# A fused attention and FFN layer: LN3's VectorE work reordered, 35 FFN products ahead of the slots instead of 30, and step 0's weight preparation and K stacking redistributed

## The chip, the cores and the metric

One core of one Trainium2 chip. TensorE is PE in the profile, its weight loads PEld, VectorE DVE, ScalarE ACT, GpSimd POOL, SyncE SP (SPq where its queue of DMAs is meant). The metric is the time of one launch on the device in microseconds (us); lower is better.

## What is computed

```python
x = L0_attn_hidden_states                                  # 16 x 512 x 512
x = x + _layernorm(_L0_attn_ref(_layernorm(x), ...))
x = x + _layernorm(_L0_ffn_ref(_layernorm(x), ...))
# attention: q = x @ Wq_down.T @ Wq_up.T, c = x @ Wkv_down.T, k and v from c per head (16 heads of 32),
#            scores * SCALE - slope * |i - j|, causal, softmax, @ v, @ Wo.T
# FFN:       weights are 4-bit codes times fp16 group scales; h = silu(x @ Wg.T) * (x @ Wu.T); y = h @ Wd.T; y / rms(y)
```

## The kernel before

Every fp32 operand is split into a high and a low fp16 part, and a product is three matmuls (high x high, high x low, low x high) that accumulate in one PSUM bank. ACT writes the high part ("high"), DVE the rest ("low", line 873).

The program is a row of steps, `step(t)` for t = 0 to 16. Step t does the attention of sequence t (`att`) and the FFN of sequence t - 1 (`ffn`); step 0 has attention alone, step 16 FFN alone, steps 1 to 15 have both. All engines run hand-written queues in a fixed order; semaphores join them.

The head of a step, on PE: transposes of the input, the output projection WO of the sequence before, C (the 128-wide latent), Q0 and Q1, K0 to K3, Q2 and Q3, V0 and V1, then the transposes of LN3's result (line 433), V2 and V3, then the first `F_FIRST` = 30 products of the FFN's up matrices (`run(0, cut(0))`). The jobs from C to V share four PSUM banks (`wide_dense`): a job opens when the job four before it has been read (`open_job`, `taken`), so Q2 waits for K0's low and Q3 for K1's. On DVE the head is: low parts of the input, LN2's moments and x1 = x + LN2 (line 972), Q0 and Q1 low, then four times LN3's `bn_stats` (line 982) ahead of a K low, the aggregation and the request for 1/sqrt (`ask_rstd`, answered by POOL, line 1080), Q2 and Q3 low, the four norms (line 788), and the low parts of their transposes. SP stacks Q and K for the slots with DMAs: 12 for the first half of Q once Q1's low is there, then 12 for K, then 12 for the rest of Q (line 1195). The FFN's jobs F0, F1, ... (12 products each, gate and up alternating) rotate through three banks: `gate(m)` frees the bank of gate job 2m, `up(m)` that of up job 2m+1, and a job opens when the one three before it is free.

After the head come 64 slots (`SLOTS`). A slot has score tiles for row maxima (`maximum`, line 505) or transposed score tiles for the exponentials (`transposed`, line 522) and a share of the FFN's products: `cut(slot)` spreads what is left after `F_FIRST` by the weights `PER_SLOT`. The slots in which ACT, DVE and POOL do `tanh(m)`, `gate(m)`, `up(m)`, `h_high` and `h_low` follow from `cut` through `up_done` and `down_done`: `tanh(m)` stands one slot behind the one that finishes its job, `gate(m)` two behind. In slot 16 ACT also takes the logarithm of the first half of the row sums, which loads an ACT table before and after; in slot 18 DVE splits the result (`lse_split`). The same comes again in slots 40 and 42.

Step 0 also prepares weights. `prepare` makes Wq from its factors; `decode(0)` turns the gate/up codes into fp8 on DVE (two masks, an OR, two masks, an OR, and the scales, on 128x1408 words), `decode(1)` does the same with the down codes (128x704), `decode_wo` makes Wo's low half. 33 `unit`s then expand the codes: POOL multiplies codes by scales (line 1090), PE transposes (line 365), ACT or DVE writes the high and DVE the low half. Nine units stand ahead of the slots of step 0, the other 24 in its slots 0 to 39.

## Time and profile before

| | us |
|---|---|
| median of 3 runs (lowest to highest) | 2552.22 (2552.08 to 2552.81) |
| the profiled execution, whole | 2549.71 |
| its span on the core | 2547.8 |
| PE busy (mean granted clock 0.985) | 2445.3 |
| DVE busy | 1523.3 |
| ACT busy | 1465.3 |
| POOL busy | 591.6 |

PE is busy for 96% of the span, so the view to read is what PE waits for, stage by stage. Matmuls are pipelined and their ends are modelled: 12 matmuls in a row start 0.216 us apart, and the last one's listed end lies some 0.16 us behind the point at which the next could start. A wait is therefore best taken from start to start.

### The profile page before, as it was taken

The page shows a single profiled execution, that of the slowest core. Times are in us where ns is not written, and L with a number is a line of the kernel's source. Part 1 is how long each engine was busy: PE and PEld are TensorE (multiplying, and loading weights), DVE is VectorE, ACT ScalarE, POOL GpSimd, SP SyncE. Part 2 cuts the span into 40 slices and gives each one's busy share as a digit, 9 for nine tenths or more (in the row PEclk, how much of TensorE's full clock was granted, in tenths as well). Part 3 has the DMA queues.
Part 4 walks back from the last instruction along what each step waited for, and adds up shares of the span by engine and source line. Part 5 has one row for each costly group of instructions (what it writes and reads, how often), then busy time and mean ns, then how long its engine had stood idle before and what let it go on. Part 6 is the DMA issues. An engine that isn't in the chain of part 4 may idle for free.

```text
span 2547.8 us, 38721 instructions
## 1 busy us (share of the span) xinstructions
PE 2445.3 (96%) x13372; PEld 1112.6 (44%) x13372; DVE 1523.3 (60%) x4300; ACT 1465.3 (58%) x3927; POOL 591.6 (23%) x648
## 2 busy tenths in 40 slices
PE   6689999999999999999999999999999999999988
PEld 3334444444444444444444444444444444444433
DVE  6856475565646657575665647556564665657442
ACT  3756556474664747566474655747566474756610
POOL 3312313123131221313122131312213122131312
PEclk9699999999999999999999999999999999999999
DMA  5020121201112020121202012120111202012000
GB/s 138 23 49 19 51 50 34 67 18 42 43 43 59 25 72 11 46 50 35 67 18 62 22 51 50 35 67 18 42 43 43 59 24 74 8 48 50 19 17 17
DMA packets 99521, 108.89 MB, mean 43 GB/s; under 512 B 22895, under 2 KB 73199, under 8 KB 99311
## 3 DMA queue, kind: packets, MB, share of 16 engines
q1 hardware_dynamic: 99326, 106.44, 15.9%
q8 instruction: 105, 1.72, 0.3%
q14 instruction: 90, 0.74, 0.1%
HBM read 38.49 MB, written 16.78 MB: 22 GB/s over the span
## 4 chain that ended last, share of the span: by engine, by line
PE 80%; DVE 7%; ACT 5%; SPq 3%; issue 2%; DMA 1%; POOL 1%; DVEq 0%; POOLq 0%
PE dense L338 58%; PE psO L538 6%; PE score L522 4%; SPq L1195 3%; PE psO L338 3%; PE low L505 3%; PE score L505 3%; DVE st_ln L777 2%; ACT arena L719 1%; PE low L522 1%; DVE arena L873 1%; DMA kst<-arena 1%; DVE low L1024 1%; ACT L650 1%; ACT L719 1%
## 5 line engine op out<-in xcount | busy, mean ns | idle before, releaser
L338 PE MATMUL dense<-arena,wgu 128*128 128x512 f16 x4224 | 999.9, 379 | 11.4 <-DVE late L886 10.2
L338 PEld LDWEIGHTS dense<-arena,wgu 128*128 128x128 f16 x4224 | 405.3, 97 | 445.2 <-DVE late L886 17.5
L338 PE MATMUL dense<-wdn,arena 128*128 128x512 f16 x2112 | 533.0, 380 | 2.6 <-POOL arena L1109 2.6
L1109 POOL TENSOR_TENSOR arena<-late,arena 128x512 f16<-128x512 f32 x176 | 203.4, 1156 | 1050.8 <-DVE arena L907 1050.8
L1024 DVE CUSTOM_DVE_ANT_0 low<-low,mmax 128x128 f32<-128x128 f32 (+3 forms) x672 | 278.7, 435 | 260.8 <-PE low L505 257.9
L719 ACT ACTIVATE arena<-score 128x512 f32<-128x512 f32 (+3 forms) x720 | 302.4, 440 | 188.6 <-PE score L522 142.2
L644 ACT ACTIVATE low<-low,ncol 128x128 f32<-128x128 f32 (+3 forms) x672 | 300.1, 447 | 136.7 <-DVE ncol L1024 128.4
L644 ACT ACTIVATE score<-score,ncol 128x384 f32<-128x384 f32 x352 | 214.0, 608 | 169.8 <-DVE ncol L1024 169.4
L338 PEld LDWEIGHTS dense<-wdn,arena 128*128 128x128 f16 x2112 | 199.2, 98 | 186.7 <-issue 11.5
L1024 DVE CUSTOM_DVE_ANT_0 score<-score,mmax 128x384 f32<-128x384 f32 x352 | 214.2, 649 | 100.3 <-PE score L505 100.0
L522 PE MATMUL score<-qst,kst 128*128 128x512 f16 (+3 forms) x784 | 218.6, 306 | 13.8 <-ACT arena L719 12.6
L1122 POOL TENSOR_SCALAR_AFFINE_SELECT arena<-arena 128x512 f32<-128x512 f32 x240 | 165.6, 690 | 280.6 <-ACT arena L719 278.7
L912 DVE TENSOR_SCALAR arena<-oc 128x512 f16<-128x512 f32 x64 | 27.3, 426 | 272.2 <-ACT oc L638 272.2
L538 PE MATMUL psO<-arena 128*32 128x512 f32 (+3 forms) x1920 | 178.7, 444 | 3.7 <-ACT oc L638 1.6
L505 PE MATMUL low<-kst,qst 125*128 125x128 f16 (+3 forms) x672 | 156.3, 277 | 12.9 <-ACT low L644 9.5
L886 DVE SCALAR_TENSOR_TENSOR late<-late,dense 128x512 f32<-128x512 f32 x176 | 120.5, 684 | 57.1 <-ACT late L629 55.8
L1024 DVE DVE_READ_ACCUMULATOR2_ANT ncol<- 128x1 f32 x1024 | 145.2, 142 | 0.2
L629 ACT ACTIVATE late<-dense 128x512 f32<-128x512 f32 x176 | 103.7, 589 | 67.3 <-PE dense L338 67.3
L894 DVE SCALAR_TENSOR_TENSOR late<-late,dense 128x512 f32<-128x512 f32 x176 | 120.3, 684 | 32.6 <-PE dense L338 32.6
L719 ACT ACTIVATE arena<-low 128x384 f32<-128x384 f32 (+3 forms) x240 | 104.3, 435 | 51.1 <-PE low L522 51.1
L644 ACT ACTIVATION_READ_ACCUMULATOR low<-low,ncol 128x1 f32 x672 | 133.2, 198 | 0.0
L522 PEld LDWEIGHTS score<-qst,kst 128*128 128x128 f16 x784 | 72.0, 98 | 138.2 <-ACT arena L719 61.1
(138 smaller groups left out, 2874.2 us busy)
## 6 DMA issues: line engine op xcount, KB each, us to landing
qst<-arena SPq DMA_DIRECT2D x384, 64.0 KB, 2.1
kst<-arena SPq DMA_DIRECT2D x192, 128.0 KB, 2.5
xin<-x SPq DMA_DIRECT2D x16, 1024.0 KB, 5.2
late<-x SPq DMA_DIRECT2D x64, 256.0 KB, 2.8
out<-late SPq DMA_DIRECT2D x64, 256.0 KB, 2.0
qst<-mrow SPq DMA_DIRECT2D x96, 8.0 KB, 1.9
wgu<-wo_t SPq DMA_DIRECT2D x1, 1024.0 KB, 7.8
wgu<-wq_down SPq DMA_DIRECT2D x1, 768.0 KB, 4.5
```

Source lines behind the costliest of these rows:

```text
L338: ins = nc.tensor.matmul(dst, w, a, start=first and k == 0, stop=last and k == len(tt) - 1)
L505: nc.tensor.matmul(mx_bank(k)[:, 0:P * (i + 1)], qst[0:P - 3, h, P * i:P * i + P], kst[0:P - 3, h, 0:P * (i + 1)], start=True, stop=True). ...
L522: ins = nc.tensor.matmul(st_bank(e)[:, 0:wide], kst[:, h, P * kt:P * kt + P], qst[:, h, P * kt:L], start=True, stop=h >= STEEP)
L538: ins = nc.tensor.matmul(psO[HD * a:HD * a + HD, P * kt:L], v[:, kt, HD * (HG * g + a):HD * (HG * g + a) + HD], prob_of(s)[:, a, 0:wide], ...
L629: nc.scalar.activation(tb[:, m % 2, :], bank(t, n)[:, :], ACT.Tanh, scale=0.5 / (S_X * S_W4)).then_inc(sem["tanh"], 1)
L644: nc.scalar.activation(mx_bank(k)[:, 0:wide], mx_bank(k)[:, 0:wide], ACT.Exp, scale=-1.0, bias=ncol[:, k:k + 1], accum_out=scol[:, k:k + 1 ...
L719: nc.scalar.activation(prob_of(e // HG)[:, e % HG, 0:wide], st_bank(e)[:, 0:wide], ACT.Exp, scale=1.0 / S_SCORE).then_inc(sem["exp"], 1)
L886: nc.vector.scalar_tensor_tensor(tb[:, m % 2, :], tb[:, m % 2, :], 1.0, bank(t, n)[:, :], ALU.add, ALU.mult).then_inc(sem["freev"], 1)
L894: nc.vector.scalar_tensor_tensor(tb[:, m % 2, :], tb[:, m % 2, :], S_H / (2 * (S_X * S_W4) ** 2), bank(t, n)[:, :], ALU.mult, ALU.mult).th ...
L1024: nc.vector.tensor_tensor_reduce(out=mx_bank(k)[:, 0:wide], in0=mx_bank(k)[:, 0:wide], in1=mmax[:, L - wide:L], scale=-1.0 / S_SCORE, scal ...
L1109: nc.gpsimd.tensor_tensor(ht[:, 1, m, :], tb[:, m % 2, :], ht[:, 0, m, :], ALU.subtract).then_inc(sem["hl"], 1)
L1122: nc.gpsimd.affine_select(out=diagonal, in_=diagonal, compare_op=ALU.is_ge, fill=0.0, base=0, pattern=[[0, HG], [1, P]], channel_multiplie ...
```

## The change

In the steps that have both halves, DVE's order changes: LN3's first two `bn_stats` stand behind Q0's low and ahead of Q1's, the third behind K0's low, the fourth behind K1's; the aggregation and the request for 1/sqrt follow at once, ahead of K2's low; the four norms stand behind Q2's low and ahead of Q3's. `F_FIRST` is 35 instead of 30.

In step 0, the decoding of the gate/up codes is cut in three: the first mask pair and OR behind the input's low parts, the second pair of masks behind C's low, the second OR and the scales behind Q0's low. The decoding of the down codes (`decode_down`) moves from the head into slot 4. Wo's low half is made by POOL in two instructions ahead of its first unit, and is no longer on DVE. The first loads are issued in another order (down codes, gate/up codes, Wo, gate/up scales, down scales). K is stacked by two queues: SP issues heads 0 and 1 of each group of four, ACT heads 2 and 3, behind its K highs and a wait for K3's low.

```diff
-F_FIRST = 30
+F_FIRST = 35
...
+        def stack(queue, dst, hi, slots, lo_g, hi_g, heads, done):
+            for slot, s in enumerate(slots):
+                for a in heads:
+                    queue.dma_start(
+                        dst[HD * slot:HD * slot + HD, :, :].rearrange("p (g a) l -> p g a l", a=HG)[:, lo_g:hi_g, a, :],
+                        qk[HD * a:HD * a + HD, hi + s, lo_g:hi_g, :]).then_inc(sem[done], 16)
...
+                    if isinstance(t, int) and t == 0:
+                        taken(act, t, j["K"] + NG - 1)
+                        stack(nc.scalar, kst, 2, (0, 0, 1), 0, NG, range(2, HG), "kstk")
                     for g in range(2, NG):
                         high(job_q(t, g), qk[:, 0, g, :], HD ** -0.5 * S_QK / (S_X * S_WQ))
...
-                decode(0)
                 for c in range(KC):
                     dve.wait_ge(s_prep_hi, c + 1)
...
-            def decode_wo():
-                dve.wait_ge(s_raw_hi, 4)
-                nc.vector.scalar_tensor_tensor(wo[:, 1, :, :].rearrange("p a b -> p (a b)"), raw[:, 9 * D:13 * D], S_W,
-                                               wo[:, 0, :, :].rearrange("p a b -> p (a b)"),
-                                               ALU.mult, ALU.subtract).then_inc(s_raw_lo, 1)
...
                 if isinstance(t, int) and t == 0:
-                    decode(1)
+                    decode(0)
...
                     low("C", 0, ct[:, 1, :], S_C / (S_X * S_W), ct[:, 0, :])
+                if isinstance(t, int) and t == 0:
+                    decode(1)
...
-                if att:
-                    for g in range(2):
-                        low("Q", g, qk[:, 1, g, :], HD ** -0.5 * S_QK / (S_X * S_WQ), qk[:, 0, g, :])
-                for g in range(NG):
-                    if ffn:
-                        dve.wait_ge(sem["add2"], val("add2", t, g + 1))
-                        link(t, nc.vector.bn_stats(st6["ln3"][:, g, :], x1[:, g, :]))
-                    if att:
-                        low("K", g, qk[:, 3, g, :], S_QK / (S_C * S_W), qk[:, 2, g, :])
-                if ffn:
+                if att:
+                    q_low(0)
+                if isinstance(t, int) and t == 0:
+                    decode(2)
+                if ffn:
+                    for i in range(2):
+                        ln3_stats(i)
+                if att:
+                    q_low(1)
+                    k_low(0)
+                if ffn:
+                    ln3_stats(2)
+                if att:
+                    k_low(1)
+                if ffn:
+                    ln3_stats(3)
                     aggregate(t, "ln3", range(NT))
                     ask_rstd("ln3")
                 if att:
-                    if isinstance(t, int) and t == 0:
-                        decode_wo()
                     for g in range(2, NG):
-                        low("Q1", g - 2, qk[:, 1, g, :], HD ** -0.5 * S_QK / (S_X * S_WQ), qk[:, 0, g, :])
+                        k_low(g)
+                if att:
+                    q_low(2)
                 if ffn:
                     dve.wait_ge(sem["rs"], val("rs", t, 2))
                     for i in range(NT):
                         normalise("ln3", xn2[:, i, :], x1[:, i, :], i).then_inc(sem["ln3"], 1)
+                if att:
+                    q_low(3)
...
+                    if isinstance(t, int) and t == 0 and slot == 4:
+                        decode_down()
...
             def unit(u):
-                pool.wait_ge(s_bits, 7 if u < 2 * MI else 14)
+                pool.wait_ge(s_bits, 7)
+                if u >= 2 * MI:
+                    pool.wait_ge(s_dbits, 7)
+                if u == 0:
+                    pool.wait_ge(s_wo_lo, 1)
...
                 if isinstance(t, int) and t == 0:
+                    pool.wait_ge(s_raw_hi, 4)
+                    flat = raw[:, 9 * D:13 * D]
+                    nc.gpsimd.tensor_scalar(flat, flat, S_W, None, ALU.mult).then_inc(s_wo_s, 1)
+                    pool.wait_ge(s_wo_s, 1)
+                    nc.gpsimd.tensor_tensor(wo[:, 1, :, :].rearrange("p a b -> p (a b)"), flat,
+                                            wo[:, 0, :, :].rearrange("p a b -> p (a b)"), ALU.subtract).then_inc(s_wo_lo, 1)
                     for u in range(RING):
                         unit(u)
...
+                        own = 2 if done == "kstk" and isinstance(t, int) and t == 0 else HG
+                        stack(nc.sync, dst, hi, slots, lo_g, hi_g, range(own), done)
```

On DVE, the head of step 1 (the same in steps 1 to 15; `dense` and `psO` are the banks of the jobs, `st_ln`, `mv_ln`, `ve_ln` LN3's moments, `arena<-late,mv_ln,rs_ln` its norm). Before, from K0's low on:

```order
242 L873 SCALAR_TENSOR_TENSOR arena<-psO,arena 128x512
243 L982 BN_STATS st_ln<-late 128x6
244 L873 SCALAR_TENSOR_TENSOR arena<-dense,arena 128x512
245 L982 BN_STATS st_ln<-late 128x6
246 L873 SCALAR_TENSOR_TENSOR arena<-dense,arena 128x512
247 L982 BN_STATS st_ln<-late 128x6
248 L873 SCALAR_TENSOR_TENSOR arena<-dense,arena 128x512
249 L784 BN_AGGR mv_ln<-st_ln 128x2 x4
250 L879 TENSOR_SCALAR ve_ln<-mv_ln 128x4
251 L873 SCALAR_TENSOR_TENSOR arena<-psO,arena 128x512
252 L873 SCALAR_TENSOR_TENSOR arena<-dense,arena 128x512
253 L788 TENSOR_SCALAR arena<-late,mv_ln,rs_ln 128x512 x4
```

After, from the first two `bn_stats` on (the rows ahead are x1's and Q0's low):

```order
240 L1011 BN_STATS st_ln<-late 128x6 x2
241 L897 SCALAR_TENSOR_TENSOR arena<-dense,arena 128x512
242 L897 SCALAR_TENSOR_TENSOR arena<-psO,arena 128x512
243 L1011 BN_STATS st_ln<-late 128x6
244 L897 SCALAR_TENSOR_TENSOR arena<-dense,arena 128x512
245 L1011 BN_STATS st_ln<-late 128x6
246 L800 BN_AGGR mv_ln<-st_ln 128x2 x4
247 L903 TENSOR_SCALAR ve_ln<-mv_ln 128x4
248 L897 SCALAR_TENSOR_TENSOR arena<-dense,arena 128x512 x2
249 L897 SCALAR_TENSOR_TENSOR arena<-psO,arena 128x512
250 L804 TENSOR_SCALAR arena<-late,mv_ln,rs_ln 128x512 x4
251 L897 SCALAR_TENSOR_TENSOR arena<-dense,arena 128x512
```

The aggregation moved ahead of K2's and K3's low, and the norms (x4) ahead of the last low of Q.

On DVE around slots 16 to 18 of step 1, where LSE is split (rows of `lcol` and `mh`). L886 is `gate`, L894 `up`, L907 `h_high`, the ISA rows row maxima. Before:

```order
344 L1024 ISA score,ncol<-score,mmax 128x512
345 L1024 ISA ncol 128x1
346 L1024 ISA low,ncol<-low,mmax 128x128
347 L1024 ISA ncol 128x1
348 L1024 ISA low,ncol<-low,mmax 128x256
349 L1024 ISA ncol 128x1
350 L922 TENSOR_TENSOR lcol<-ncol,lcol 128x32
351 L924 TENSOR_SCALAR mh<-lcol 128x32
352 L926 SCALAR_TENSOR_TENSOR lcol<-lcol,mh 128x32
353 L929 TENSOR_SCALAR mh<-lcol 128x32
354 L931 TENSOR_TENSOR mh<-lcol,mh 128x32
355 L886 SCALAR_TENSOR_TENSOR late<-late,dense 128x512
```

After (L910 is `gate`, L918 `up`):

```order
342 L1071 ISA score,ncol<-score,mmax 128x512
343 L1071 ISA ncol 128x1
344 L910 SCALAR_TENSOR_TENSOR late<-late,dense 128x512
345 L1071 ISA low,ncol<-low,mmax 128x128
346 L1071 ISA ncol 128x1
347 L1071 ISA low,ncol<-low,mmax 128x256
348 L1071 ISA ncol 128x1
349 L946 TENSOR_TENSOR lcol<-ncol,lcol 128x32
350 L948 TENSOR_SCALAR mh<-lcol 128x32
351 L950 SCALAR_TENSOR_TENSOR lcol<-lcol,mh 128x32
352 L953 TENSOR_SCALAR mh<-lcol 128x32
353 L955 TENSOR_TENSOR mh<-lcol,mh 128x32
```

`gate(6)`, which stood behind the split in slot 18, now stands in slot 17, ahead of slot 18's tiles; on ACT its `tanh(6)` moves from slot 17 to slot 16, ahead of the table loads.

On DVE in step 0, from the low halves of the small weights on. Before (L831 to L840 are `decode`, L809 Wq's low, L873 the lows of the input and of C):

```order
9 L805 SCALAR_TENSOR_TENSOR vup<-wgu,vup 128x512
10 L831 TENSOR_SCALAR arena<-arena 128x1408
11 L832 TENSOR_SCALAR arena<-arena 128x1408
12 L834 TENSOR_TENSOR late<-arena 128x1408
13 L836 TENSOR_SCALAR arena<-arena 128x1408
14 L837 TENSOR_SCALAR arena<-arena 128x1408
15 L839 TENSOR_TENSOR late<-arena 128x1408
16 L840 TENSOR_SCALAR late<-arena 128x88
17 L809 SCALAR_TENSOR_TENSOR wq<-dense,wq 128x512 x3
18 L809 SCALAR_TENSOR_TENSOR wq<-psO,wq 128x512
19 L873 SCALAR_TENSOR_TENSOR arena<-low,arena 128x512 x2
20 L873 SCALAR_TENSOR_TENSOR arena<-score,arena 128x512 x2
```

After:

```order
10 L824 SCALAR_TENSOR_TENSOR wq<-dense,wq 128x512 x3
11 L824 SCALAR_TENSOR_TENSOR wq<-psO,wq 128x512
12 L897 SCALAR_TENSOR_TENSOR arena<-low,arena 128x512 x2
13 L897 SCALAR_TENSOR_TENSOR arena<-score,arena 128x512 x2
14 L833 TENSOR_SCALAR arena<-arena 128x1408
15 L834 TENSOR_SCALAR arena<-arena 128x1408
16 L836 TENSOR_TENSOR late<-arena 128x1408
17 L897 SCALAR_TENSOR_TENSOR ct<-psO,ct 128x512
18 L839 TENSOR_SCALAR arena<-arena 128x1408
19 L840 TENSOR_SCALAR arena<-arena 128x1408
20 L897 SCALAR_TENSOR_TENSOR arena<-dense,arena 128x512
21 L843 TENSOR_TENSOR late<-arena 128x1408
```

The input's lows no longer stand behind a decode, and C's low now stands behind the first piece of it.

## Rows read from the trace of the kernel before

**Rows 1.** Busy time, slots of step 0: span, PE, PEld, DVE, ACT, POOL; PE clock, DMA, GB/s.

```profile
60.10:155.70 95.60, 67.77 (x379) 32.48 (x380) 67.86 (x202) 71.59 (x215) 35.34 (x40) 0.75 0.11 31
```

**Rows 2.** Waits of PE, whole span: engine, line, whom for; us, times, longest.

```profile
PE low L433 <- DVE arena L788: 20.5, 16, 10.9
PE score L522 <- ACT arena L719: 12.6, 22, 3.1
PE dense L338 <- DVE late L886: 10.2, 15, 0.7
...
PE low L505 <- DMA kst<-arena: 3.2, 7, 0.7
```

**Rows 3.** Timeline, head of step 7: start, us, engine, line, out<-in, xcount [idle <-releaser].

```profile
1083.31 2.11 PE L338 MATMUL dense<-ct,kup 128*128 128x512 f16 x9
...
1083.57 0.69 DVE L873 SCALAR_TENSOR_TENSOR arena<-dense,arena 128x512 f16<-128x512 f32 x1 [1.17 <-PE psO L338]
...
1084.28 7.71 SPq L1195 DMA_DIRECT2D qst<-arena  x12
...
1085.51 2.76 PE L338 MATMUL psO<-arena,wq 128*128 128x512 f16 x12
...
1089.59 1.01 POOL L1080 TENSOR_TENSOR rs_ln<-ve_ln,half 128x4 f32<-128x4 f32 x1 [11.34 <-DVE ve_ln L879]
...
1090.69 1.46 PE L338 MATMUL dense<-vup,ct 128*128 128x512 f16 x6
...
1092.04 8.53 SPq L1195 DMA_DIRECT2D kst<-arena  x12
1092.20 1.91 DVE L788 TENSOR_SCALAR arena<-late,mv_ln,rs_ln 128x512 f32<-128x512 f32 x4
...
1092.80 0.44 PE L433 MATMUL low<-id,arena 128*128 128x128 f32 x2 [0.64 <-DVE arena L788]
...
1096.07 6.63 PE L338 MATMUL dense<-arena,wgu 128*128 128x512 f16 x30
```

**Rows 4.** Timeline, slot 18 of the same step.

```profile
1138.32 1.89 PE L338 MATMUL dense<-arena,wgu 128*128 128x512 f16 x8
...
1139.34 0.59 ACT L629 ACTIVATE late<-dense 128x512 f32<-128x512 f32 x1
...
1140.14 0.68 DVE L886 SCALAR_TENSOR_TENSOR late<-late,dense 128x512 f32<-128x512 f32 x1
...
1140.88 0.39 PE L338 MATMUL dense<-arena,wgu 128*128 128x512 f16 x1 [0.68 <-DVE late L886]
```

**Rows 5.** Timeline, step 0 ahead of its slots.

```profile
18.68 0.89 DVE L831 TENSOR_SCALAR arena<-arena 128x1408 int32<-128x1408 int32 x1
...
22.55 1.94 ACT L672 ACTIVATE wo<-wgu 128x2048 f16<-128x2048 f32 x1
...
25.33 0.20 DVE L840 TENSOR_SCALAR late<-arena 128x88 f32<-128x88 f16 x1
...
30.23 0.52 DVE L831 TENSOR_SCALAR arena<-arena 128x704 int32<-128x704 int32 x1
30.37 5.19 PE L338 MATMUL psO<-arena,wkv 128*128 128x512 f16 x12 [8.51 <-DVE arena L873]
...
33.95 0.18 DVE L840 TENSOR_SCALAR late<-arena 128x44 f32<-128x44 f16 x1
...
51.99 1.50 PE L365 MATMUL dense<-id,arena 128*128 128x128 f32 x12 [0.89 <-ACT arena L692]
```

**Rows 6.** Timeline, VectorE and GpSimd on SBUF at once, end of step 1.

```profile
281.46 1.95 DVE L788 TENSOR_SCALAR xin<-xin,mv_ln,rs_ln 128x512 f32<-128x512 f32 x2
281.62 1.50 POOL L1115 TENSOR_TENSOR late<-late 128x512 f32<-128x512 f32 x1 [0.68 <-DVE late L954]
```

**Rows 7.** Groups of POOL by form: line, op, names, shapes, xcount, busy us, mean ns, idle.

```profile
L1109 POOL TENSOR_TENSOR arena<-late,arena 128x512 f16<-128x512 f32 x176 | 203.4, 1156 | 1050.8 <-DVE arena L907 1050.8
L1122 POOL TENSOR_SCALAR_AFFINE_SELECT arena<-arena 128x512 f32<-128x512 f32 x240 | 165.6, 690 | 280.6 <-ACT arena L719 278.7
```

More of the change, by code:

```diff
@@ L234, in layer_program @@
         s_dn = ctx.enter_context(nc.semaphore("s_dn"))
+        s_dn_sc = ctx.enter_context(nc.semaphore("s_dn_sc"))
+        s_dbits = ctx.enter_context(nc.semaphore("s_dbits"))
+        s_wo_s = ctx.enter_context(nc.semaphore("s_wo_s"))
+        s_wo_lo = ctx.enter_context(nc.semaphore("s_wo_lo"))
         s_id = ctx.enter_context(nc.semaphore("s_id"))
@@ L375, in step @@
                 if isinstance(t, int) and t == 1:
[L377 removed]
+                    pe.wait_ge(s_wo_lo, 1)
                     pe.wait_ge(s_prep_lo, KC + UNITS)
@@ new lines, in decode_down @@
+            def decode_down():
+                ts = nc.vector.tensor_scalar
+                words, low3, sign = packed[:, GUW:W], bits1[:, 0:DNW], packed[:, 0:DNW]
+                dve.wait_ge(s_dn, 16)
+                dve.wait_ge(s_bits, 7)
+                ts(low3, words, 0x07070707, 2, ALU.bitwise_and, ALU.logical_shift_left).then_inc(s_dbits, 1)
+                ts(sign, words, 0x08080808, 4, ALU.bitwise_and, ALU.logical_shift_left).then_inc(s_dbits, 1)
+                dve.wait_ge(s_dbits, 2)
+                nc.vector.tensor_tensor(codes[:, 0, GUW:W], low3, sign, ALU.bitwise_or).then_inc(s_dbits, 1)
+                dve.wait_ge(s_dbits, 3)
+                ts(low3, words, 0x70707070, 2, ALU.bitwise_and, ALU.logical_shift_right).then_inc(s_dbits, 1)
+                ts(sign, words, -0x7F7F7F80, None, ALU.bitwise_and).then_inc(s_dbits, 1)
+                dve.wait_ge(s_dbits, 5)
+                nc.vector.tensor_tensor(codes[:, 1, GUW:W], low3, sign, ALU.bitwise_or).then_inc(s_dbits, 1)
+                dve.wait_ge(s_dn_sc, 16)
+                ts(sc32[:, 2 * MI * GROUPS:NSC], sc16[:, 2 * MI * GROUPS:NSC], FP8_SCALE * S_W4, None,
+                   ALU.mult).then_inc(s_dbits, 1)
@@ L1192, in step @@
                         taken(sp, t, last)
-                        for slot, s in enumerate(slots):
-                            for a in range(HG):
-                                sp.dma_start(
-                                    dst[HD * slot:HD * slot + HD, :, :].rearrange("p (g a) l -> p g a l", a=HG)[:, lo_g:hi_g, a, :],
-                                    qk[HD * a:HD * a + HD, hi + s, lo_g:hi_g, :]).then_inc(sem[done], 16)
+                        own = 2 if done == "kstk" and isinstance(t, int) and t == 0 else HG
+                        stack(nc.sync, dst, hi, slots, lo_g, hi_g, range(own), done)
                     for part in range(2):
```

53 lines of the change are left out of this document (29 added, 24 removed).

## The prediction

> **What bounds the kernel now.** I read the waits of PE over the span first [rows 2], then the timeline of one middle step, then step 0 by itself. PE works nearly all the time, so what the change can give is what PE waits, and the waits have a pattern. The one for LN3's norm and the one for a gate come in each of the 15 double steps (the norm's 10.9 us in the last step, which has no attention, is a 16th), the one for an exponential comes once a step too, and the wait for K's stack comes 7 times, 3.2 us in all, one of them in step 0. Step 0 is another matter: in its slots DVE is busy 67.86 of 95.60 us and PE runs at a mean granted clock of 0.75, so PE does not set its end [rows 1]. In the first third of those slots DVE has hardly a gap, later ACT is as busy.
>
> I cost each wait from start to start, with 0.216 us from one product to the next (a row of 12 lists 2.76 with a modelled tail of some 0.16 [rows 3]).
>
> **The double steps: LN3.** The two first `bn_stats` go where DVE stood idle for 1.17 us ahead of Q1's low [rows 3]. In the old order each of these and each low took 0.60 us of DVE, so two need 1.19: Q1's low stays where it is, at 1083.57, and so does the start of SP's stacking at 1084.28. K0's low then follows at 1084.17, not at 1084.86. PE had nine K products from 1083.31, so Q2 could open at 1085.25 and opened at 1085.51 [rows 3]. Gain (a): 0.26 us.
> The aggregation waits for the fourth `bn_stats` right behind it, which the K3 low used to cover; I charge 0.1. K2's and K3's lows come some 0.1 us later than before, which nobody feels: V0 and V1 want them three us later, and SP is busy with Q's 12 DMAs until 1092.04. The request for 1/sqrt goes out at 87.2, POOL answers in 1.01 us [rows 3], so at 88.3. Q2's product ends 0.26 earlier, ACT copies it, its low runs 88.8 to 89.4, and the norms 89.4 to 91.3 (1.91 for four [rows 3]). PE arrives with V0 and V1 done at 1090.69 + 6 x 0.216 - 0.26 = 1091.72 and finds all four. Before, it could have come at 1091.98 and started at 1092.80. Gain (b): 0.82 us. What is late next: Q3's low (about 91.3 to 91.9), wanted by V3 at 94.2, so nothing.
>
> **The double steps: 35 products ahead.** PE is now 1.08 us earlier at the head's end, but K's stack is not: SP's chain of 7.71 and 8.53 us starts at the same point [rows 3]. Five products more take 5 x 0.216 = 1.08, so PE meets slot 0 where it did, and the occasional waits for K's stack stay what they were. Without the five, the gain of (a) and (b) would be handed back there; this edit has no price of its own but is their cover.
> It also shifts the slots. Product 180 opens F15 and needs `gate(6)`. That gate runs at 1140.14 because tanh(6), queued behind ACT's table loads, ends only at 1139.9 and the LSE split stands ahead of it; PE could have gone on at 1138.32 + 8 x 0.216 = 1140.05 and did at 1140.88 [rows 4]. With the new `cut`, job 12 ends one slot earlier, tanh(6) stands in slot 16 ahead of the loads and the gate in slot 17, over an us before PE wants it. Gain 0.83. Next late is F16, now the first product of slot 20 while `up(6)` stands in slot 19: by the pattern of a slot with the wide tiles that is a tie, for which I take off 0.08. Gain (c): 0.75 us.
> Against it: ahead of the first pair of tiles in slot 42 PE waits 0.54 for an exponential behind the second table load (15 of the 22 waits of that name [rows 2]). Slot 40 has one product less now, so that wait grows. Loss (d): 0.2 us.
> Sum: 0.26 + 0.82 + 0.75 - 0.2 = 1.63, times 15 = 24.4 us. Step 16 has no attention, its order of LN3 does not change and neither does its 10.9.
>
> **Step 0, the head.** The input's lows no longer stand behind a decode of 6.9 us (18.68 to 25.53 [rows 5]): they end near 23.9 (30.37 less 6.9, and half a us since ACT's copies then come last), and PE starts C there. The idle time ahead of C shrinks from 8.51 us to 2. C's 12 products took 5.19 us, the same number takes 2.76 elsewhere [rows 3, 5]; that is the lower of the two clocks after a long idle stretch. I take 2.6 for them now. Everything from there follows some 9 us earlier if DVE keeps pace: the first unit's transposes at 43.6 instead of 51.99 [rows 5], since nine units of POOL's pace then follow in both versions, and K's stack (6 DMAs on each queue, about 0.7 us each) is there before they end.
> But DVE may not keep pace. POOL now works 128x2048 elements twice, from the end of ACT's Wo copy at 24.5 [rows 5] on. No trace shows these forms at this size; by the nearest rows, 128x512 takes 0.69 with one input and 1.16 with two [rows 7], times four 2.8 and 4.6, together 7.4 us (I stay with that; up to 9.2 if both run at the two-input rate). In the same time DVE's decode pieces run from SBUF to SBUF, 6.9 us of them. And such pairs do not overlap here: at 281.46 two norms, 0.48 us each where four take 1.91 [rows 3], took 1.95, since the second ran only after POOL's addition of 1.50 that lies between [rows 6]. So I serialise: masks, POOL's scaling 24.8 to 27.5, a mask, POOL's subtraction 28.3 to 32.9, and the OR behind it to 34.6. C's low, queued behind that OR, is 7 us late (35.2); K0 waits for it, PE has done C and Q0, Q1 (36 products) by 31.7 and idles to 35.2, DVE has two masks, Q0's low, an OR and Q1's low to do, and K3's low ends near 42.2. ACT then issues six DMAs (0.64 each by SP's 7.71 for 12 [rows 3]: 3.9 us), in front of Q2's high. V's last copy ends near 49.8 and the units start at 49.9: of 8.4 us gained 2.1 remain.
> The Trainium skill states this as a rule in "SBUF — State Buffer", section "Who interferes with whom": VectorE in a two-port mode or with two SBUF inputs and GpSimd take one shared pair of ports in turn, for a whole instruction each. Without it the head would give 8.4 us, with it 2.1; the row at 281.46 agrees with the rule, and my sum goes by that row.
>
> **Step 0, the slots.** `decode_down` used to run 30.23 to 34.13, 3.9 us [rows 5], beside PE's C product: free. Now it stands in slot 4, where DVE is the bound, so all of it counts, and one unit of POOL (two inputs, 1.1 us by [rows 7]) gets between its pieces: 5.0 us, bounds 3.9 and 6.
> Sum of step 0: -2.1 + 5.0 = 2.9 us slower; between 4.5 faster (no contention: 8.4 - 3.9) and 6 slower.
>
> **Forecast.** -24.4 + 2.9 = -21.5. Against the profiled execution's 2549.71 that is 2528.2; the median lies 2.5 above it (2552.22), so 2530.7, say 2531 us.
>
> **Rivals.**
> A: VectorE and GpSimd do not hinder each other in the head of step 0. For it: units and VectorE's row maxima run side by side in the slots. Against it: [rows 6]. Step 0 gives 4.5 instead of costing 2.9: 2523.3 us.
> B: the gate's wait does not go but moves, to F16 or to another job that the new cuts bring to the edge. For it: F16 is a tie, and this wait was itself one slot's shift away. Against it: no other job came near a wait before. It costs (c), 11 us: 2542.
> C: LN3 gives nothing, because the head's end is K's stack after all: its last DMA sometimes hangs (six of the 15 double steps wait), and PE's gain turns into longer waits at slot 0. It takes (a) and (b), 16 us: 2547.
> D, slower: the two `bn_stats` push Q1's low. Their 1.19 us against an idle 1.17 has no slack; SP's chain starts on that low, and each us of delay is an us of idle PE at slot 0 in 15 steps. It outweighs the gains from a delay of 1.43 us on (24.4 - 2.9 = 21.5 over 15 steps), that is if a `bn_stats` took 1.3 instead of 0.6; at 1.8 us of delay the time is 2531 + 27 = 2558. Nothing in the profile shows such a duration.
> E: no change, for instance if POOL's 1/sqrt comes late so that (b) stays and F16 takes (c) while step 0 costs 6: within 5 us of 2552.
>
> **How the numbers follow.** Forecast 0.51, A 0.20, B 0.14, C 0.07, D 0.04, E 0.04. What a measurement can tell from no change is 0.2%, 5 us. Faster: 0.92; same 0.04; slower 0.04. The range takes in A at the lower end with an us or two for step 0's unknown durations, and B at the upper one: 2521 to 2543.
>
> **What the changed profile would show.** (a) and (b): no wait of PE for the norm in steps 1 to 15, only the last step's 10.9. (c): no wait for the gate in slot 18; one of under 0.1 in slot 20 at most. (d): the wait for the exponential at some 0.75. K's stack: still a wait in about six steps. Double steps 1.6 us shorter each. Step 0: decode pieces stretched or displaced where POOL's two long instructions run, PE idle ahead of K0, units from about 50 us, and a block of some 5 us of decode in slot 4. I am wrong if the double steps shrink by under a us, if Q1's low and with it SP's first stack start later against the head's products, or if the ORs start at once beside POOL.

## The result and the profile after

The changed kernel takes 2531.47 us (2530.07 to 2532.58), the kernel before 2552.15 on the same chip: a ratio of 0.992, with a 95% interval of 0.9903 to 0.9937. The forecast was 2531. The profiled execution took 2531.45 us, its span is 2528.9 against 2547.8.

The waits of PE over the whole span after the change (engine, line, whom for; us, times, longest):

```profile
PE score L534 <- ACT arena L735: 17.1, 22, 3.1
PE score L517 <- ACT score L656: 13.3, 15, 4.9
PE low L445 <- DVE arena L804: 10.9, 1, 10.9
...
PE dense L350 <- DVE arena L897: 5.6, 3, 3.9
...
PE low L517 <- DMA kst<-arena: 3.5, 9, 0.9
```

Against [rows 2]: the wait for LN3's norm has gone from 16 times to once, the last step's. The row for the gate is no longer there. The wait for an exponential rose from 12.6 to 17.1, K's stack from 3.2 to 3.5. Two more changed, both in step 0. The 5.6 us for low parts are new. The wait for a score bank (L517, `row_sum` on ACT) was 8.3 us before:

```profile
PE score L505 <- ACT score L644: 8.3, 13, 2.2
```

It is 13.3 now, 4.9 of it at once, behind a row maximum that came late.

The head of step 7 (start, us, engine, line, out<-in, count, idle and who ended it):

```profile
1079.18 2.11 PE L350 MATMUL dense<-ct,kup 128*128 128x512 f16 x9
...
1079.44 0.69 DVE L897 SCALAR_TENSOR_TENSOR arena<-dense,arena 128x512 f16<-128x512 f32 x1
...
1080.16 7.71 SPq L307 DMA_DIRECT2D qst<-arena  x12
...
1081.12 2.75 PE L350 MATMUL psO<-arena,wq 128*128 128x512 f16 x12
...
1085.22 1.91 DVE L804 TENSOR_SCALAR arena<-late,mv_ln,rs_ln 128x512 f32<-128x512 f32 x4
...
1087.60 0.38 PE L445 MATMUL low<-id,arena 128*128 128x128 f32 x2
```

Measure from the nine K products, as in [rows 3]. Q1's low still stands 0.26 us behind their start and SP's first stack 0.98 behind it (0.97 before), so nothing was pushed. Q2 opens after 1.94 instead of 2.20. LN3's transposes start after 8.42 instead of 9.49, with no idle time ahead of them.

The place of the gate's wait, step 7, slots 16 to 18:

```profile
1130.69 0.59 ACT L641 ACTIVATE late<-dense 128x512 f32<-128x512 f32 x1
...
1131.30 1.28 ACT L662 ACT_TABLE_LOAD   x1
...
1132.38 0.68 DVE L910 SCALAR_TENSOR_TENSOR late<-late,dense 128x512 f32<-128x512 f32 x1
...
1134.49 0.19 DVE L946 TENSOR_TENSOR lcol<-ncol,lcol 128x32 f32<-128x32 f32 x1
```

tanh(6) now ends as the table load begins, and the gate runs 2.1 us ahead of the LSE split; in [rows 4] it came behind both.

Step 0 ahead of its slots:

```profile
24.86 0.88 DVE L833 TENSOR_SCALAR arena<-arena 128x1408 int32<-128x1408 int32 x1
25.00 2.76 PE L350 MATMUL psO<-arena,wkv 128*128 128x512 f16 x12 [2.06 <-DVE arena L897]
25.66 0.88 DVE L834 TENSOR_SCALAR arena<-arena 128x1408 int32<-128x1408 int32 x1
25.66 6.12 POOL L1190 TENSOR_SCALAR wgu<-wgu 128x2048 f32<-128x2048 f32 x1 [10.60 <-ACT wo L684]
26.57 4.95 DVE L836 TENSOR_TENSOR late<-arena 128x1408 int32<-128x1408 int32 x1
...
31.45 0.68 DVE L897 SCALAR_TENSOR_TENSOR ct<-psO,ct 128x512 f16<-128x512 f32 x1
31.86 4.06 POOL L1192 TENSOR_TENSOR wo<-wgu,wo 128x2048 f16<-128x2048 f32 x1
32.05 4.63 DVE L839 TENSOR_SCALAR arena<-arena 128x1408 int32<-128x1408 int32 x1
...
32.78 0.81 PE L350 MATMUL dense<-ct,kup 128*128 128x512 f16 x3
...
33.42 0.81 PE L350 MATMUL psO<-ct,kup 128*128 128x512 f16 x3
...
36.59 0.88 DVE L840 TENSOR_SCALAR arena<-arena 128x1408 int32<-128x1408 int32 x1
37.99 1.61 DVE L843 TENSOR_TENSOR late<-arena 128x1408 int32<-128x1408 int32 x1
38.13 1.46 PE L350 MATMUL dense<-ct,kup 128*128 128x512 f16 x3 [3.89 <-DVE arena L897]
...
40.34 10.19 SPq L307 DMA_DIRECT2D qst<-arena  x12
...
41.63 4.10 PE L350 MATMUL dense<-arena,wq 128*128 128x512 f16 x12
...
43.30 4.30 ACTq L307 DMA_DIRECT2D kst<-arena  x6
...
51.83 1.50 PE L377 MATMUL dense<-id,arena 128*128 128x128 f32 x12 [0.92 <-ACT arena L708]
```

C starts 5.4 us earlier than in [rows 5]. Then comes GpSimd: the OR (L836) is listed with 4.95 us and a mask (L839) with 4.63, where their twins L843 and L840 take 1.61 and 0.88. PE does K0 and K1 (32.78, 33.42) and stands ahead of K2 until 38.13. By 51.83 all but 0.16 us of the lead is gone.

The decoding in slot 4, and PE's wait behind it:

```profile
68.39 0.52 DVE L853 TENSOR_SCALAR arena<-arena 128x704 int32<-128x704 int32 x1
...
69.37 1.61 DVE L856 TENSOR_TENSOR late<-arena 128x704 int32<-128x704 int32 x1
71.02 1.25 DVE L858 TENSOR_SCALAR arena<-arena 128x704 int32<-128x704 int32 x1
...
73.63 0.56 DVE L1071 CUSTOM_DVE_ANT_0 score<-score,mmax 128x384 f32<-128x384 f32 x1
...
75.01 0.50 PE L517 MATMUL score<-kst,qst 125*128 125x384 f16 x1 [4.93 <-ACT score L656]
```

From 68.39 to 73.63 DVE takes no row maximum, the exponential behind it (`row_sum`) comes late, and PE stands for 4.93 us.

### The profile page after: what moved, and what is told of

It reads as the page before. It is cut to its first block, busy times and chain, and to the rows that moved or that the text cites. A ratio compares the mean times of both kernels' runs of the same rounds, so it can differ in the third digit from the quotient of the medians.

```text
span 2528.9 us, 38723 instructions
## 1 busy us (share of the span) xinstructions
PE 2439.4 (96%) x13372; PEld 1116.3 (44%) x13372; DVE 1525.8 (60%) x4299; ACT 1464.9 (58%) x3927; POOL 602.6 (24%) x650
## 4 chain that ended last, share of the span: by engine, by line
PE 83%; DVE 5%; SPq 4%; ACT 4%; issue 2%; DMA 1%; POOL 0%; POOLq 0%; DVEq 0%
PE dense L350 60%; PE psO L550 7%; SPq L307 4%; PE score L534 4%; PE low L517 3%; PE psO L350 3%; PE score L517 3%; PE low L534 1%; DMA kst<-arena 1%; DVE arena L897 1%; ACT L662 1%; ACT L735 1%; ACT low L656 1%; ACT arena L735 1%; DVE late L998 1%
## 5 line engine op out<-in xcount | busy, mean ns | idle before, releaser
L1071 DVE CUSTOM_DVE_ANT_0 score<-score,mmax 128x384 f32<-128x384 f32 x352 | 214.1, 648 | 101.1 <-PE score L517 99.7
L534 PE MATMUL score<-qst,kst 128*128 128x512 f16 (+3 forms) x784 | 218.0, 305 | 18.4 <-ACT arena L735 17.1
L550 PE MATMUL psO<-arena 128*32 128x512 f32 (+3 forms) x1920 | 178.2, 443 | 3.9 <-POOL arena L1176 1.7
L517 PE MATMUL low<-kst,qst 125*128 125x128 f16 (+3 forms) x672 | 156.2, 277 | 13.4 <-ACT low L656 9.6
L910 DVE SCALAR_TENSOR_TENSOR late<-late,dense 128x512 f32<-128x512 f32 x176 | 120.3, 683 | 50.9 <-ACT late L641 49.6
L918 DVE SCALAR_TENSOR_TENSOR late<-late,dense 128x512 f32<-128x512 f32 x176 | 120.1, 683 | 32.6 <-PE dense L350 32.6
```

The lines of the kernel that those rows point to most:

```text
L517: nc.tensor.matmul(mx_bank(k)[:, 0:P * (i + 1)], qst[0:P - 3, h, P * i:P * i + P], kst[0:P - 3, h, 0:P * (i + 1)], start=True, stop=True). ...
L534: ins = nc.tensor.matmul(st_bank(e)[:, 0:wide], kst[:, h, P * kt:P * kt + P], qst[:, h, P * kt:L], start=True, stop=h >= STEEP)
L550: ins = nc.tensor.matmul(psO[HD * a:HD * a + HD, P * kt:L], v[:, kt, HD * (HG * g + a):HD * (HG * g + a) + HD], prob_of(s)[:, a, 0:wide], ...
L910: nc.vector.scalar_tensor_tensor(tb[:, m % 2, :], tb[:, m % 2, :], 1.0, bank(t, n)[:, :], ALU.add, ALU.mult).then_inc(sem["freev"], 1)
L918: nc.vector.scalar_tensor_tensor(tb[:, m % 2, :], tb[:, m % 2, :], S_H / (2 * (S_X * S_W4) ** 2), bank(t, n)[:, :], ALU.mult, ALU.mult).th ...
L1071: nc.vector.tensor_tensor_reduce(out=mx_bank(k)[:, 0:wide], in0=mx_bank(k)[:, 0:wide], in1=mmax[:, L - wide:L], scale=-1.0 / S_SCORE, scal ...
```

## The experiments

Some numbers come from the start of each step, taken as PE's first input transpose. A **period** is the time from one such start to the next. Before, the 14 periods of steps 1 to 15 sum to 2119.3 us and the shortest is 151.10. After, they sum to 2095.6 and the shortest is 149.33. Each kernel was timed beside the kernel before on its own chip:

| kernel | us (lowest to highest) | ratio, 95% interval |
|---|---|---|
| changed kernel | 2531.47 (2530.07 to 2532.58) | 0.992, 0.9903 to 0.9937 |
| the same, other chip (a_again) | 2527.30 (2525.91 to 2531.57) | 0.9916, 0.99 to 0.9933 |
| c1_steps_only | 2525.45 (2523.37 to 2525.99) | 0.9901, 0.9884 to 0.9917 |
| s1_before_f35 | 2539.56 (2535.94 to 2540.15) | 0.9952, 0.9936 to 0.9969 |
| s3_after_f30 | 2552.99 (2547.92 to 2555.73) | 1.0007, 0.9998 to 1.0016 |
| s6_three_stats_first | 2533.82 (2532.82 to 2536.20) | 0.9936, 0.9921 to 0.9951 |
| s4_fill_exp_wait | 2530.22 (2529.11 to 2531.87) | 0.9916, 0.9901 to 0.993 |
| e1_wo_low_vectore | 2521.25 (2520.48 to 2522.75) | 0.9886, 0.9871 to 0.9901 |
| e5_wo_apart | 2523.28 (2520.59 to 2524.82) | 0.9894, 0.9879 to 0.9909 |
| e2_down_in_head | 2525.43 (2522.25 to 2525.66) | 0.9899, 0.9884 to 0.9914 |
| e3_both | 2518.58 (2517.78 to 2518.98) | 0.9874, 0.9858 to 0.9891 |
| e4_one_queue | 2529.93 (2529.49 to 2530.54) | 0.9921, 0.9907 to 0.9936 |
| b1_both_f36 | 2518.93 (2518.57 to 2520.31) | 0.9879, 0.9864 to 0.9894 |

The repeated run sets the yardstick:

> The changed kernel itself, on the chip of this group: 2531 us within 2, arena transposes at about 51 us, step 1 at 158 to 160 us.

It came out 4 us lower than the first time, below the range expected, with 5.7 us between its lowest and its highest run; the units' transposes start at 50.52 and step 1 at 157.49. The first execution had 51.83 and 159.99. So single executions of one program lie 2.5 us apart at the end of step 0, and its waits for K's stack were 2, of 1.0 us in all, where the first had 9 of 3.5. Differences of 2 or 3 us in step 0, or of a few waits at slot 0, are not read below as effects.

### Each part by itself

The double steps alone: the kernel before, with VectorE's new order in LN3 (as in the change's diff) and

```diff
-F_FIRST = 30
+F_FIRST = 35
```

> The kernel before with the double steps' part of the change alone: LN3's new order on VectorE and F_FIRST 35; step 0 is the old one in every instruction. If the two parts simply add, step 1 starts where it did (153.8 us), the periods are the changed kernel's (149.5 to 149.7 on the mean), and the time is 24 to 26 us below the kernel before: 2524 to 2526 on a chip where that takes 2550. That is 2 to 6 us below the changed kernel, so the rearrangement of step 0, as it was made, costs time. Rival: the new step 0 is worth something that the step's start does not show (a full granted clock later, or a lead in the stacking), and this version is no faster than the changed kernel: 2527 to 2531.

2525.45 us, as the first theory had it: 24.9 below the kernel before. The shortest period is 149.33, the changed kernel's, and the 14 sum to 2093.3; step 1 starts at 155.14, against 157.49 to 159.99 with the new step 0. The parts add, and step 0 as rearranged costs 4 to 5 us (ratios 0.992 and 0.9916 against 0.9901). The intervals of these ratios overlap; the starts of step 1 do not: 153.69 to 155.14 in the three executions with the old step 0, 157.49 to 159.99 in the five that have the new one as changed.

`F_FIRST` alone, in the kernel before, by the same two lines:

> The kernel before with F_FIRST = 35 and nothing else. Theory: the gate's wait goes (0.75 us a step), the wait for an exponential grows by 0.2, the norm's wait of 0.64 (0.82 from start to start) stays, PE meets slot 0 1.08 us later so that K's stack is never waited for (3 to 4 us in all): 2552 - 8.3 - 3 = 2541. Rival (the gain is all LN3's and F_FIRST only covers it): 2549 to 2552.

The period is 150.53 to 150.66 in all steps. The shortest fell by 0.56 us, where the forecast had 0.55 for (c) and (d). No gate is waited for, the exponential costs 0.76 a step, and LN3's norm 0.64 as before. By the ratio the time is 12 us below before's, near the 11.3 of the first theory: the waits for K's stack went from the double steps as well, and PE met slot 0 at 40.90 us into its step instead of 39.81 to 40.68, behind the last copy. LN3's order is what remains, 150.54 - 149.33 = 1.21 us.

And LN3's order without the five products (the changed kernel with `F_FIRST = 30`):

> The changed kernel with F_FIRST = 30. Theory: PE reaches slot 0 1.08 us earlier and waits there for K's stack in every double step, so LN3's gain is handed back, and the gate's wait returns: 1.63 us a step, 24 us, total 2556, above the kernel before by step 0's 6 us less its own share. Rival (LN3's gain does not depend on the five products): only the gate returns, 2542.

Its waits of PE:

```profile
PE low L517 <- DMA kst<-arena: 14.8, 13, 1.5
...
PE dense L350 <- DVE late L910: 10.2, 15, 0.7
```

2552.99 us, no gain in the total. The transposes of LN3 start at 29.00 into the step, as in the changed kernel, against 30.07 before. But slot 0 starts at 39.86 on the median against 39.89 before. PE waits there for K's stack, and the gate's wait is back. The total includes the new step 0, though: step 1 starts at 158.47 against 153.81, 4.7 us later, and the 14 periods sum to 2115.1 against 2119.3, 4.2 less. So the new order on VectorE alone keeps 0.30 us a step. It gives 0.9 in the two steps without a wait for K's stack (periods of 150.18 and 150.23) and hands most of that back in the others.

### The slack around LN3's moments

```diff
-                    for i in range(2):
+                    for i in range(3):
                         ln3_stats(i)
...
-                if ffn:
-                    ln3_stats(2)
```

> The changed kernel with the third bn_stats of LN3 also ahead of Q1's low, in each of the 15 double steps. Theory (VectorE's idle time there is used up by two, Q1's low starts SP's chain of stacking, and slot 0 waits for its end): Q1's low 0.6 us later, K's stack 0.6 later, a wait of about 0.6 us at slot 0 in every double step, total + 15 x 0.6 = 9 us, 2540. Rival (SP's chain has slack): no wait, 2531.5.

The idle gap ahead of Q1's low was 1.17 us, and three `bn_stats` take 1.8. The SP chain did start later, 1.49 us behind the start of the nine K products (1079.10) instead of 0.98:

```profile
1078.11 1.87 DVE L1011 BATCH_NORM_STATS2 st_ln<-late 128x6 f32<-128x512 f32 x3
1079.89 0.67 DVE L897 SCALAR_TENSOR_TENSOR arena<-dense,arena 128x512 f16<-128x512 f32 x1
...
1080.59 7.72 SPq L307 DMA_DIRECT2D qst<-arena  x12
```

Yet the shortest period rose only from 149.33 to 149.56, and the mean of the 14 by 0.33 us against the first execution of the changed kernel (150.01 against 149.69) and 0.52 against the second (149.49), with 8 waits for K's stack of 4.1 us in all. The rise in an undisturbed step does not come through SP's chain. K0's low is later too, so Q2 opens 2.18 us behind the K products instead of 1.94, and slot 0 comes at 39.93 instead of 39.70, without a wait for a copy. The chain's delay of 0.51 us shows, if at all, in the other steps. The time is 2.4 us above the changed kernel's by the medians and 4 by the ratios, not 9. So rival D's price, a us of idle PE for each us of delay, was too high for a small delay.

### The wait for an exponential

```diff
-PER_SLOT[17], PER_SLOT[18], PER_SLOT[41] = 11, 10, 11
+PER_SLOT[17], PER_SLOT[18], PER_SLOT[41] = 11, 10, 14
+PER_SLOT[42], PER_SLOT[43] = 0.2, 3.8
```

> The changed kernel with 14 FFN products in slot 41, none in slot 42 and 3 in slot 43 instead of 11, 3 and 3; the cuts from slot 44 on are the same. Three products more stand ahead of PE's wait of 0.75 us for an exponential behind ACT's second table load. Theory 1 (only that one exponential is late): the wait goes, 0.65 us a step stays gained, total 2531.5 - 9.8 = 2522. Theory 2 (ACT is late for the whole group of tiles behind the table load): the wait moves to the tiles of slot 43, which have no products ahead of them now, and the total stays within 3 us of 2531.5.

The changed kernel (first three rows) and this one (the last three), slots 41 and 42 of step 7:

```profile
1170.63 2.54 PE L350 MATMUL dense<-wdn,arena 128*128 128x512 f16 x11
...
1173.45 0.34 PE L534 MATMUL low<-qst,kst 128*128 128x384 f16 x1
1174.54 0.34 PE L534 MATMUL score<-qst,kst 128*128 128x384 f16 x1 [0.75 <-ACT arena L735]
```

```profile
1168.14 3.18 PE L351 MATMUL dense<-wdn,arena 128*128 128x512 f16 x14
...
1172.07 0.34 PE L535 MATMUL score<-qst,kst 128*128 128x384 f16 x1
1172.55 0.34 PE L535 MATMUL score<-qst,kst 128*128 128x384 f16 x1 [0.15 <-ACT arena L736]
```

The listed wait shrank from 0.75 to 0.15, and the shortest period stayed where it was (149.34 against 149.33). The tiles of slots 42 and 43 now start 0.38 to 0.48 us apart, near ACT's pace (exponentials of 0.50). From the first product of slot 41 to the second group of products with V (L551 at 1173.90, before L550 at 1176.48) it takes 5.76 us instead of 5.85. So the second theory holds: ACT is late for the whole group, and term (d) is no loss that this other place of the products wins back.

### Wo's low half on GpSimd

Two runs keep the rest of the change. In the first (e1_wo_low_vectore) VectorE makes Wo's low half again, ahead of Q2's low:

```diff
+                if isinstance(t, int) and t == 0:
+                    dve.wait_ge(s_raw_hi, 4)
+                    nc.vector.scalar_tensor_tensor(wo[:, 1, :, :].rearrange("p a b -> p (a b)"), raw[:, 9 * D:13 * D], S_W,
...
-                    nc.gpsimd.tensor_scalar(flat, flat, S_W, None, ALU.mult).then_inc(s_wo_s, 1)
```

> The changed kernel with one part undone: Wo's low half is made by VectorE again, ahead of Q2's low in step 0, and GpSimd makes none. Theory (VectorE and GpSimd take turns on SBUF in step 0's head, and that is where its 7 us went): the three stretched decode instructions return to 0.9, 1.6 and 0.9 us, C's low comes at 28.3 instead of 31.5, Q1's low at 33.5 instead of 40.2, the first unit's transposes near 44.7 instead of 51.8, total 2531.5 - 7.1 = 2524. Rival (the decode pieces and the second queue's DMAs are themselves too long for the head): the units still start near 51, total 2531. Rival (K's stack then sets slot 0, since SP's twelve Q DMAs took 10.2 us): slot 0 gains less than the units, total about 2528.

In its trace the decode instructions take 1.62 and 0.88 us again, C's low stands at 28.91 and the units start at 45.92 (44.7 was expected). The time is 2521.25, some 3 us less than the 2524 of the theory.

In the second (e5_wo_apart) GpSimd keeps both instructions and begins them when the decoding is done:

```diff
+                    pool.wait_ge(s_bits, 7)
                     pool.wait_ge(s_raw_hi, 4)
                     flat = raw[:, 9 * D:13 * D]
```

> The changed kernel, with the two GpSimd instructions for Wo's low half held back until VectorE has finished decoding Wqkv: the same work on the same engine, apart in time. Theory 1 (the two engines slow each other on SBUF in step 0): VectorE's decode instructions fall back to about 0.9, 1.6 and 0.9 us, GpSimd's scaling shows its undisturbed time (6.12 us listed beside the decode), the arena transposes start near 45 to 46 us as with Wo's low half on VectorE (45.92), and the time is 6 to 8 us below the changed kernel's on the same chip. Theory 2 (GpSimd's subtraction ends too late for its units, whatever VectorE does): the arena transposes stay near 51 us and the time is within 1 us of the changed kernel's.

Its rows on VectorE and GpSimd:

```profile
26.61 1.62 DVE L836 TENSOR_TENSOR late<-arena 128x1408 int32<-128x1408 int32 x1
...
29.14 0.88 DVE L839 TENSOR_SCALAR arena<-arena 128x1408 int32<-128x1408 int32 x1
...
33.63 5.38 POOL L1191 TENSOR_SCALAR wgu<-wgu 128x2048 f32<-128x2048 f32 x1 [18.58 <-DVE late L844]
33.71 1.34 DVE L897 SCALAR_TENSOR_TENSOR arena<-dense,arena 128x512 f16<-128x512 f32 x2 [0.25 <-PE dense L350]
...
39.09 4.07 POOL L1193 TENSOR_TENSOR wo<-wgu,wo 128x2048 f16<-128x2048 f32 x1
```

Nothing but the time of the two GpSimd instructions differs. The OR is back at 1.62 and the mask at 0.88, and the units start at 44.96 instead of 50.52 to 51.83 (45.92 with VectorE doing the work). The time falls by 4 us against the repeated run on the same chip, where 6 to 8 was expected; the ratios differ by 5.6 us and their intervals overlap a little (0.9879 to 0.9909, 0.99 to 0.9933). Step 1 starts 5.0 us earlier. So the stretched decoding is caused by the overlap and not by the amount of GpSimd's work, and it delays the units by 5.6 to 6.9 us. That the two engines hinder each other, as forecast, is shown, and rival A is out.

The rule of the Trainium skill that the forecast set beside [rows 6] ("SBUF — State Buffer", section "Who interferes with whom") has another side: a VectorE instruction with at most one input from SBUF does not contend, as long as it runs outside the two-port modes. The trace agrees: the lows at 33.71, with one input from PSUM and one from SBUF, take 0.67 each beside the scaling of 5.38 us. One input alone is not enough, since the mask L839 has one too and was held. It took 0.88 us undisturbed for 1408 elements, where the OR took 1.62; that it ran in a two-port mode would fit, and no run here tests it.

### The down codes in slot 4

```diff
+                if isinstance(t, int) and t == 0:
+                    decode_down()
...
-                    if isinstance(t, int) and t == 0 and slot == 4:
-                        decode_down()
```

(the first two lines stand behind the lows of K and ahead of Q2's)

> The changed kernel with the decoding of the down codes moved from slot 4 of step 0 into its head, behind K's lows, where VectorE stood idle for 5.1 us while ScalarE issued DMAs. Theory (in the slots of step 0 VectorE is the bound, so the block of 5.2 us counts in full, and in that idle stretch it is free): the units start at 51.8 as before, the slots of step 0 are 5 to 6 us shorter, total 2526. Rival (the slots of step 0 are bound by ACT and the later exponentials, which absorb it): the transposes of step 1 stay near 160 us, total 2531. Rival (it delays Q2's low and the units): head 2 to 4 us longer, total 2528.

Both changes at once, Wo's low half on VectorE and `decode_down` in the head (e3_both):

> Both together: Wo's low on VectorE and the down codes decoded in the head, behind K's lows. If the two parts are independent, 7.1 + 5.3 less about 1 us (the down decode now ends behind the point at which Q2's low could run): units near 45.7 us, total 2520. If VectorE has no room for both in the head, 2524 to 2526.

The slots of step 0, from slot 0 to some 2 us past step 1's start (columns as in [rows 1]), in the changed kernel and in the one with `decode_down` in the head:

```profile
59.10:161.88 102.78, 68.22 (x382) 32.42 (x381) 73.67 (x210) 71.44 (x215) 36.96 (x41) 0.73 0.09 26
```

```profile
58.80:155.74 96.94, 67.87 (x382) 32.35 (x380) 68.66 (x203) 71.57 (x215) 36.19 (x41) 0.75 0.08 26
```

DVE's busy time falls by 5.01 us and the stretch by 5.84. The starts in us, one execution each (C: its first product; units: their first transposes; slots: from slot 0 to step 1):

| | C | units | slot 0 | step 1 | slots |
|---|---|---|---|---|---|
| before | 30.37 | 51.99 | 60.17 | 153.81 | 93.6 |
| c1_steps_only | 30.47 | 52.40 | 60.41 | 155.14 | 94.7 |
| changed | 25.00 | 51.83 | 59.18 | 159.99 | 100.8 |
| a_again | 24.11 | 50.52 | 57.88 | 157.49 | 99.6 |
| e1_wo_low_vectore | 24.11 | 45.92 | 53.26 | 153.70 | 100.4 |
| e5_wo_apart | 25.03 | 44.96 | 52.88 | 152.54 | 99.7 |
| e2_down_in_head | 23.71 | 51.52 | 58.86 | 153.85 | 95.0 |
| e3_both | 24.49 | 45.48 | 52.83 | 150.05 | 97.2 |

With the decoding in slot 4 the slots take 99.6 to 100.8 us, without it 93.6 to 97.2. The instructions that PE had as cover in the head were moved to where VectorE sets the pace. Both repairs together give 2518.58 us, 12.9 us under the changed kernel by the medians and 10.7 by the ratios of the repeated run. That beats both kernels. By the ratios against 0.992 it gains 11.7, where the two single gains are 8.7 and 5.4; their intervals don't tell 11.7 from the sum. The slots of e3 took 2.2 us more than those of e2, in one execution each. The mean granted clock in them is 0.72 against 0.75; why it is lower there was not tested.

### Two queues for K's stack

The changed kernel without

```diff
-                    if isinstance(t, int) and t == 0:
-                        taken(act, t, j["K"] + NG - 1)
-                        stack(nc.scalar, kst, 2, (0, 0, 1), 0, NG, range(2, HG), "kstk")
```

and with all four heads issued by SP:

> The changed kernel, with K's stack copies of step 0 issued by SP's queue alone. If two queues bring the copies sooner as forecast (SP's 12 for Q 10.2 us from 40.3, then 12 for K 8 us, landing 2.6 us after, so slot 0 at about 61 instead of 59.2), step 0 is 1 to 2 us longer. Rival: ScalarE is free of the issues, Q2's high halves and the units come 2 to 3 us earlier, SP's Q copies are issued in 8 us again, and slot 0 stands within 0.5 us of where it was: within 1 us of the changed kernel's time.

```profile
39.21 9.04 SPq L307 DMA_DIRECT2D qst<-arena  x12
48.30 7.71 SPq L307 DMA_DIRECT2D kst<-arena  x12
...
57.88 0.34 PE L517 MATMUL low<-kst,qst 125*128 125x128 f16 x2 [0.27 <-DMA kst<-arena]
```

For slot 0 the rival holds: it starts at 57.88, to the hundredth where the repeated changed kernel has it. The second queue has the copies there early, but PE can't come before its units are done, which takes GpSimd's pace. Without it PE just waits for the last copy, for 0.27 us. The rest of the rival did not come: the units start at 50.10, only 0.4 us earlier, and SP's 12 issues for Q did not fall to 8 us. The time is 2529.93, on the same chip 2.6 us above the repeated changed kernel (1.3 by the ratios), where the rival had under 1. That lies within the changed kernel's 2525.91 to 2531.57, and of the 3.8 us between the two spans 2.1 stand behind the start of step 15 (275.16 us to the end against 273.09). So a loss of 1 to 2 us in all is not excluded, and none is seen at slot 0.

SP's 12 issues for Q took 9.04 us here with ACT's queue idle, and 9.18 and 10.19 beside it. In the kernel before they took 8.27 in step 0, and blocks of 12 took 7.63 to 9.27 in the changed kernel's double steps. So ACT's issues aren't the main cause of the slow row, which stays open. The Trainium skill ("DMA: Bandwidth & Descriptors", section "Issuing engines are not separate DMA queues") says that a second issuing engine saves only the sequencer's time for the issues. The run fits that: the second queue spared SP six issues, and here nobody wanted that time.

### One product more

The version of e3_both with `F_FIRST = 36`:

> The version with Wo's low half on VectorE and Wdown decoded in the head (2518.6 us), and F_FIRST 36 in place of 35. If the short waits for K's stack copies at slot 0 (9 of them, 3.5 us in all in the changed kernel) exist because TensorE gets there 0.2 us too early, one more product ahead of slot 0 fills them: the waits fall under 1 us in all and the time is 1 to 3 us below 2518.6. Rival: the added matmuls only replace waiting, or F3 opening at slot 0 waits for the gate (as it did in the kernel before, 0.68 us a step): 0 to +8 us.

2518.93 us, the same as e3_both. The waits for K's stack fell from 4, of 1.4 us, to 2, of 0.7, but the shortest period rose from 149.34 to 149.55: slot 0 now starts at 39.92 into every undisturbed step instead of 39.70, and the slots behind it take as long as before (109.63 against 109.64) with one product less. Why they don't shrink was not tested. The 14 periods sum to 2095.3 against 2093.5, so the product costs a little more than it wins back. The total is the same because step 1 started 1.9 us earlier in this execution, which is within the scatter seen above. 36 is no better than 35.

## Why the prediction was right, point by point

- **(a) and (b), LN3's order: 1.08 us a step.** In the trace LN3's transposes start 1.07 us earlier behind the K products (8.42 against 9.49), 0.26 of it at Q2 as forecast. Between them and the FFN's products there is another 0.11: 1087.60 to 1090.76 is 3.16 us, and in [rows 3] 1092.80 to 1096.07 is 3.27. It lies in the eight pairs of transposes, of which the first is listed with 0.44 instead of 0.38; its cause was not looked for. The whole part is 1.21 by the run with `F_FIRST` alone.
- **Five products as cover.** Right: without them the double steps keep 0.30 us each of some 1.7, and step 0's cost takes that up (2552.99 us). PE meets slot 0 at 39.70 in an undisturbed step, 39.81 before.
- **(c) and (d), the gate and the exponential: 0.55.** Measured 0.56 by the run with `F_FIRST` alone. The gate's wait is gone with none at F16; the exponential's is 0.75, as forecast.
- **K's stack: "a wait in about six steps".** It varies from one execution to the next: 9 waits of 3.5 us, then 2 of 1.0, of the same program. The 14 periods gave 23.7 us in the first execution and 26.5 in the second; that is 25.4 and 28.4 for 15, where the forecast was 24.4, and the steps' part alone measured 24.9 by the median.
- **Step 0: +2.9, the step that came out low.** By the ratios it cost 4 to 5 us, in the two traces 6.2 and 3.7 by step 1's start. The head gave 1.0 and 2.3 us at slot 0 where 2.1 was forecast. The slots cost 7.2 and 6.0 where 5.0 was. The decoding block was sized rightly (5.24); around it PE lost the rest, which no run takes apart, while its clock was granted at 0.73 in the slots instead of 0.75 [rows 1].
- **Inside the head**, several terms were wrong and partly cancelled. GpSimd's scaling was sized at 2.8 us from an instruction with one input [rows 7]. It takes 5.38 undisturbed and 6.12 as listed, above the upper bound of 4.6 that I gave it. The subtraction (4.6 forecast) takes 4.06. And the order of the serialised pieces was another: I held C's low until 35.2, behind an OR behind the subtraction. In fact the OR was held beside the scaling, and C's low got through between GpSimd's two instructions, at 31.45. The mask next to the subtraction was held instead, and Q0's low came behind it. So PE did not idle ahead of K0, as the forecast had it (31.7 to 35.2): K0 and K1 ran at 32.78 and 33.42, and the idle time stands ahead of K2, which waits for Q0's low, until 38.13 (3.89 us). Behind that idle time the granted clock is 0.50 (1.2 GHz) from 38.0 to 43.5, where it was 1.00 from 27.6 to 34.0; it is back at 1.00 by 45.5. Q2's 12 products take 4.10 instead of 2.75 for it. So the units start at 51.83, not 49.9.
- **Rivals.** A fell with the stretched instructions, which went back when e5 took the overlap away. That e5's 2523.28 us is A's 2523.3 is a coincidence: A had step 0 give 4.5 us, and step 1 starts 1.3 earlier than before in e5 (152.54 against 153.81), since its slots cost 6.1 and not 3.9. B fell with the vanished row of the gate. C came true only in the kernel with 30 products ahead. D fell with Q1's low at 0.26 us behind the K products, as before. E did not come.
- **The total.** The mechanisms were right and the size of the double steps too. That 2531.47 meets 2531 so closely is luck: the double steps gave 0.5 to 4 us more than forecast, step 0 cost 1 to 3 more, and the same program took 2527.30 on another chip.

## What to carry to other kernels

A lead won on one engine is worth what waits at the next rendezvous: move work into it in the same edit, and look up what the copies behind it need. An instruction that is moved off a busy engine is only free if its new engine doesn't share a path to memory with the old one at that time; if it does, hold it until the other is idle, which cost one wait here and gave 4 to 6 us. And work that preparation can hide under TensorE's products should not be moved to a stretch in which its own engine sets the pace, however short that piece looks.
